# A five-stage block on one core: every hardware loop written out, and three PSUM banks each for scores and for transposes in the decayed attention

## The reference

```python
x = x + attn_a(_layernorm(x), ...)   # mamba2: projection, conv of 4 taps, silu, state-space scan, gated rmsnorm
x = x + ffn(_layernorm(x), ...)      # 2 x (local attention, windows of 64, 8 heads of 64; gated MLP, hidden 341)
x = x + attn_b(_layernorm(x), ...)   # full attention, 16 heads of 8, scores times a distance decay
x = x + ffn(_layernorm(x), ...)      # the same weights again
```

```python
scores = jnp.einsum('bhsd,bhtd->bhst', q, k) / jnp.sqrt(D)        # 512 x 512 a head
scores = scores * jnp.exp(-jnp.abs(distance_decay[0]) * dist)
out = jnp.einsum('bhst,bhtd->bhsd', jax.nn.softmax(scores, axis=-1), v)
```

## Time and profile before

| what | value |
|---|---|
| time, median of 3 runs | 2386.45 us (2385.03 to 2386.71) |
| profiled execution, its time | 2385.01 us |
| its span on the core | 2383.2 us |
| mean granted TensorE clock | 0.97 |
| instructions | 60302 |
| busy shares of the span | PE 92%, PEld 63%, DVE 68%, ACT 63%, POOL 70% |
| parts in the trace (us from the start) | mamba to 293, t0 to 1045, decayed attention to 1636, t1 to the end |

### The profile page before, as it was taken

One profiled execution on the slowest core, in us unless ns is written; L12 is line 12 of the kernel. 1 busy time (PEld: TensorE's weight loads), 2 busy tenths in 40 slices (PEclk: granted clock), 3 DMA queues, 4 the chain that ended last, 5 costly groups with the idle time before them and its releaser, 6 DMA issues. The chain is left out here.

```text
span 2383.2 us, 60302 instructions
## 1 busy us (share of the span) xinstructions
PE 2184.3 (92%) x19744; PEld 1490.5 (63%) x19760; DVE 1627.2 (68%) x3905; ACT 1489.7 (63%) x4130; POOL 1679.1 (70%) x1712
## 2 busy tenths in 40 slices
PE   6998789998989999859999999998999978999979
PEld 4766557776557777535655656564777755677755
DVE  5777578886557777537666667675878745777755
ACT  3556368887358887325655556554888843888853
POOL 5777788886168888228777777766889822888842
PEclk8999899999999999889999999998999999999999
DMA  4000011111111111112111111101111112111101
GB/s 111 1 0 1 6 27 34 40 37 30 48 36 36 36 34 33 27 58 58 54 42 34 52 53 37 49 21 25 28 34 40 43 23 51 36 34 36 39 21 50
DMA packets 121250, 86.69 MB, mean 36 GB/s; under 512 B 85560, under 2 KB 102160, under 8 KB 118800
## 3 DMA queue, kind: packets, MB, share of 16 engines
q1 hardware_dynamic: 119248, 82.70, 14.3%
q10 hardware_dynamic: 1856, 2.23, 0.3%
HBM read 30.38 MB, written 8.39 MB: 16 GB/s over the span
## 5 line engine op out<-in xcount | busy, mean ns | idle before, releaser
L1319 DVE CUSTOM_DVE_ANT_0 store<-bank,store 128x512 f32<-128x512 f32 x512 | 340.1, 689 | 170.2 <-PE bank L1165 108.6
L1403 POOL TENSOR_SCALAR store<-store 128x512 f32<-128x512 f32 x512 | 349.7, 694 | 149.5 <-DVE store L1319 147.4
L1276 ACT ACTIVATE store<-bank 128x512 f32<-128x512 f32 x512 | 287.1, 603 | 251.2 <-PE bank L1174 247.7
L730 ACT ACTIVATE store<-bank,store 128x128 f32<-128x128 f32 x1024 | 364.2, 378 | 68.5 <-DVE store L860 68.4
L1010 POOL TENSOR_TENSOR store<-store 128x16 f32<-128x16 f32 x128 | 372.5, 2910 | 26.6 <-DVE store L856 26.6
L1004 POOL TENSOR_TENSOR store<-store 128x512 f32<-128x512 f32 x256 | 321.0, 1275 | 85.0 <-DVE store L847 83.7
L1174 PEld LDWEIGHTS bank<-store 128*128 128x128 f32 x2048 | 241.4, 142 | 130.4 <-ACT store L1276 74.1
L1174 PE MATMUL bank<-store 128*128 128x128 f32 x2048 | 298.3, 278 | 0.0
L519 PE MATMUL bank<-store 128*128 128x512 f32 x512 | 270.1, 615 | 7.1 <-DVE store L835 6.6
L1019 POOL TENSOR_TENSOR store<-store 128x512 f32<-128x512 f32 x256 | 261.5, 1043 | 17.4 <-POOL store L1010 11.4
L860 DVE TENSOR_REDUCE store<-bank 128x4 f32<-128x512 f32 x256 | 165.0, 686 | 130.4 <-PE bank L553 130.4
(11 more groups left out here) (199 smaller groups left out, 4457.3 us busy)
## 6 DMA issues: line engine op xcount, KB each, us to landing
store<-store SPq DMA_DIRECT2D x256, 128.0 KB, 2.3
store<-parts SPq DMA_DIRECT2D x96, 192.0 KB
parts<-store SPq DMA_DIRECT2D x16, 384.0 KB, 3.6
store<-store SPq DMA_DIRECT2D x128, 32.0 KB
store<-store SPq DMA_DIRECT2D x128, 31.8 KB
store<-store SPq DMA_DIRECT2D x32, 127.0 KB
store<-in_L_ffn_wqkv_dram SPq DMA_DIRECT2D x4, 768.0 KB, 4.6
out_dram<-store SPq DMA_DIRECT2D x8, 256.0 KB, 2.5
```

The source lines that it names most:

```text
L730: last = nc.scalar.activation(prob[:, e, b, :], bank[3 + e][:, b * P:(b + 1) * P], ACT.Exp, bias=nmax[:, e, b:b + 1], accum_out=psums[:, h ...
L1276: nc.scalar.activation(AT[:, h % 4, c, :], bank[2 + c][:, :], ACT.Exp, scale=-1.0).then_inc(aexp_done, 1)
L1319: nc.vector.tensor_tensor_reduce(out=S[:, h % 4, t, :], in0=bank[t % 2][:, :], in1=decay[:, off:off + L], scale=1.0, scalar=-3.0e38, op0=A ...
L1403: nc.gpsimd.tensor_scalar(s_, s_, -1.0, amax[:, h % 4, t:t + 1], ALU.mult, ALU.add).then_inc(shifted_done, 1)
```

## The change

All `Fori` loops on all engines become Python loops: the same instructions in the same order on each engine, with constants in place of registers, no register arithmetic and no branches, in a program that is several times longer. In the decayed attention the six banks that scores and turns share are divided three and three in place of two and four: score n waits for scale n-3, turn n for exp n-3. The tile's bank is now its running number modulo 3. Nothing else is moved, added or taken out. The diff, cut to one loop of each kind and all of the bank edits:

```diff
@@ -322,6 +322,7 @@
         PREP_LOADS = 8
         MAMBA_LOADS, FOLD_LOADS = 11, 3
         COMBOS = 2 * PARTS
+        SCORE_BANKS, TURN_BANKS = 3, 3
         HALF = HA // 2 * L
         FIRST = 2 * TPS
         LN_START, LN_STEPS = 2 - (B - 1), B - 1
...
@@ -348,7 +349,7 @@
         credits = ((exp_done, 2), (pT_done, 2), (wo_added, 1), (rot_done, 2), (roped_done, 4),
                    (qkT_done, 2), (v_ready, 1), (o_done, SLOTS), (ss_done, 1), (xT_done, TPS),
                    (hidden_ready, 2), (down_added, 1),
-                   (scaled_done, 2), (aexp_done, TPS), (at_done, 16), (ao_ready, 1), (av_out, TPS),
+                   (scaled_done, SCORE_BANKS), (aexp_done, TURN_BANKS), (at_done, 16), (ao_ready, 1), (av_out, TPS),
                    (xt_ready, 1), (lt_ready, 1), (mm_ready, 1), (mixed, 1), (gT_ready, 1), (fuse_added, 1))
 
         def start_pool(pool):
...
@@ -479,7 +480,7 @@
                         stage_shifted(sp, 0, q0, j)
                     meet(sp, 2 * l + meets)
                     load_ff(sp, l)
-                with sp.Fori(0, B - 1) as s:
+                for s in range(0, B - 1):
                     if l == 0:
                         sp.wait_ge(ln_ready, B * norm + s + 2)
                     for j in range(TPS):
...
@@ -677,7 +678,7 @@
                 for i in range(2):
                     project_qk(q0, 2, i)
                 attention_sequence(q0, False, True)
-                with pe.Fori(1, B - 1) as s:
+                for s in range(1, B - 1):
                     attention_sequence(q0 + s, True, True)
                 attention_sequence(q0 + (B - 1), True, False)
                 weigh_values(q0 + (B - 1), TPS - 1)
...
@@ -1064,17 +1065,17 @@
                 finish_qk(q0, 0)
                 finish_qk(q0, 1)
                 if l == 0:
-                    with pool.Fori(0, B - 2) as s:
+                    for s in range(0, B - 2):
                         attention_sequence(s, q0 + s, True, True)
                     attention_sequence(B - 2, q0 + (B - 2), True)
                 else:
-                    with pool.Fori(0, B - 1) as s:
+                    for s in range(0, B - 1):
                         attention_sequence(s, q0 + s, True)
                 attention_sequence(B - 1, q0 + (B - 1), False)
                 ff_rstd(q0, 0)
                 ff_rstd(q0 + 1, 1)
                 meet(pool, l * 2 + meets + 1)
-                with pool.Fori(0, B - 2, 2) as s:
+                for s in range(0, B - 2, 2):
                     for odd in range(2):
                         ff_rstd(q0 + s + 2 + odd, odd)
                         if last_layer:
...
@@ -1162,7 +1163,7 @@
                     pe.wait_ge(combos_in[1], (q + 1) * (16 * COMBOS))
                 h, t = k // TPS, k % TPS
                 pe.wait_ge(scaled_done, 64 * q + k + 1)
-                nc.tensor.matmul(bank[t % 2][:, :], QC[0:COMBO, h, t * P:(t + 1) * P], KC[0:COMBO, h, :],
+                nc.tensor.matmul(bank[(64 * q + k) % SCORE_BANKS][:, :], QC[0:COMBO, h, t * P:(t + 1) * P], KC[0:COMBO, h, :],
                                  start=True, stop=True).then_inc(score_done, 1)
 
             def turn(q, h, c):
...
@@ -1171,12 +1172,12 @@
                     pe.wait_ge(shifted_done, 64 * q + 4 * h + 4)
                 pe.wait_ge(aexp_done, 64 * q + 4 * h + c + 1)
                 for t in range(TPS):
-                    last = nc.tensor.transpose(bank[2 + c][:, t * P:(t + 1) * P], S[:, h % 4, t, c * P:(c + 1) * P], ident)
+                    last = nc.tensor.transpose(bank[SCORE_BANKS + (64 * q + 4 * h + c) % TURN_BANKS][:, t * P:(t + 1) * P], S[:, h % 4, t, c * P:(c + 1) * P], ident)
                 last.then_inc(at_done, 1)
 
             def weigh(q, g, c):
 
-                pe.wait_ge(aexp_done, 64 * q + 16 * g + c + 17)
+                pe.wait_ge(aexp_done, 64 * q + 16 * g + c + 13 + TURN_BANKS)
                 if c == 0:
                     pe.wait_ge(ao_ready, 4 * q + g + 1)
                     if g == 0:
...
@@ -1273,7 +1274,7 @@
                     act.wait_ge(at_done, 64 * q + 4 * h + c + 17)
                     if h % 4 == 0:
                         act.wait_ge(av_out, 16 * q + h + c + 1)
-                    nc.scalar.activation(AT[:, h % 4, c, :], bank[2 + c][:, :], ACT.Exp, scale=-1.0).then_inc(aexp_done, 1)
+                    nc.scalar.activation(AT[:, h % 4, c, :], bank[SCORE_BANKS + (64 * q + 4 * h + c) % TURN_BANKS][:, :], ACT.Exp, scale=-1.0).then_inc(aexp_done, 1)
 
             def copy_oT(q, g):
                 act.wait_ge(av_out, 16 * q + 4 * g + 8)
...
@@ -1316,7 +1317,7 @@
                 dve.wait_ge(score_done, 64 * q + 4 * h + t + 1)
                 hold(dve)
                 off = (TPS - 1 - t) * P
-                nc.vector.tensor_tensor_reduce(out=S[:, h % 4, t, :], in0=bank[t % 2][:, :], in1=decay[:, off:off + L],
+                nc.vector.tensor_tensor_reduce(out=S[:, h % 4, t, :], in0=bank[(64 * q + 4 * h + t) % SCORE_BANKS][:, :], in1=decay[:, off:off + L],
                                                scale=1.0, scalar=-3.0e38, op0=ALU.mult, op1=ALU.max,
                                                accum_out=amax[:, h % 4, t:t + 1]).then_inc(scaled_done, 1)
 
...
@@ -1363,7 +1364,7 @@
 
             nc.vector.memset(bank[6][:, :], 0.0)
             sequence(0, False, True, True)
-            with dve.Fori(1, B - 2) as q:
+            for q in range(1, B - 2):
                 sequence(q, True, True, True)
             sequence(B - 2, True, True)
             sequence(B - 1, True, False, False, True)
...
@@ -1397,7 +1398,7 @@
                     nc.gpsimd.tensor_tensor(apart[:, t, 2, :], arest[:, t, :], apart[:, t, 1, :], ALU.subtract).then_inc(apart_ready, 1)
 
             def subtract_max(q, h, t):
-                pool.wait_ge(scaled_done, 64 * q + 4 * h + t + 3)
+                pool.wait_ge(scaled_done, 64 * q + 4 * h + t + 1 + SCORE_BANKS)
                 hold(pool)
                 s_ = S[:, h % 4, t, :]
                 nc.gpsimd.tensor_scalar(s_, s_, -1.0, amax[:, h % 4, t:t + 1], ALU.mult, ALU.add).then_inc(shifted_done, 1)
```

28 lines of the change are left out of this document (14 added, 14 removed).

## The result

| what | before | after |
|---|---|---|
| time, median (range) | 2386.58 us (2385.03 to 2388.57), 4 runs | 2357.37 us (2353.88 to 2359.44), 4 runs |
| profiled execution, its span | 2385.01, 2383.2 us | 2358.81, 2357.0 us |
| instructions | 60302 | 54563 |

The changed kernel takes 0.9876 of the time before (95% interval 0.9859 to 0.9893), 29.2 us less. The prediction was 2361 us, 2347 to 2376. Lines of kernel.py after stand one further down: L1320 is the L1319 of before.

What follows compares the result with a forecast made beforehand. Outside the mamba PE's queue was taken as the bound, so only its idle time could come back: 9.2 + 5.9 + 14.4 - 2.3 - 1.5 = 25.7 us off 2385.0, giving 2359.3; as a median 2361, range 2347 to 2376.

Steps and rivals of the forecast that it cites:

- DVE's loop edge: Decayed attention: DVE's four jumps back delay the next score 1.91 us each; written out, 7.6 us gained, 9.2 with clock.
- The clock part: Decayed attention: PE's clock stood at 0.57 of full for 4.0 us after the last edge; 1.6 us counted as gain.
- POOL's registers: Transformer's attention: POOL works out wait values late; written out, 3.9 us gained in second layers, 2.0 in first, 5.9 together.
- MLP 0, SP 0: MLP's loops gain nothing because PE has no idle time; SP's gain nothing because its DMAs land well ahead.
- Mamba 0, within 1: Mamba's loops: written-out sequences have the same chain of small steps, so 0 gain, with 1 us on either side.
- The banks: Decayed attention: third score bank gains 14.4 us of PE waits; one turn bank less costs 2.3 us (1.5 to 6).
- Long code: Straight-line code makes some starts late, mostly in the decayed attention: a loss of 1.5 us, between 0 and 4.
- the case's own range: Whole kernel, main forecast: banks 11 to 16, loops 12 to 17, losses 2 to 8 us, giving 2352 to 2372.
- A third bank of no use: Rival, decayed attention: DVE is full where PE waits, so only the loops' gain is left, 2375 us; chance 0.10.
- Register work counts for more: Rival, attention stages: sequencers cause all remaining PE stalls, about 20 us more gain over 28 sequences, 2341 us; chance 0.08.
- ACT's pace: Rival, decayed attention: exps at 0.5 us against turns at 0.44 bound the turns, losing 23 us, 2384; chance 0.05.
- Code fetch: Rival, long code: PE gaps with no releaser every 10 to 15 us would show it; chance 0.05.

Runs made afterwards that it cites:

- the leaner kernel: Changed kernel's banks, but only nine loops written out (decayed PE, ACT, DVE; POOL's transformer attention; mamba's four): 2354.58 us, ratio 0.9863 to the kernel before.
- the repeat: The changed kernel measured once more with nothing altered: 2355.92 us, ratio 0.9869 to the kernel before.

## Why the prediction was right

**DVE's loop edge**, 7.6 us and 1.6 of clock. Right in mechanism and size: 2.0 us an edge against 1.91, and 8.5 us by the medians of the run with this edit alone. The clock part was one execution's, as the traces with 70.0 to 70.6 us in all four looped sequences show; without it the term is 7.6 to 8.

**POOL's registers**, 5.9 us. The second layers' 0.28 us a sequence is exact (34.11 to 33.83). The first layers' half share of it, a guess without a row, measured 0.13 to 0.16, which was luck; it was taken for 14 sequences, where the loops there hold 12, 0.3 us too much. The four layers: 1495.4 to 1497.1 us in the seven traces with POOL's loop, 1490.0 to 1492.2 in the seven with it written out, on average 5.2 us less.

**MLP 0, SP 0.** Rounds of 8.27 us in both. SP's loops were not tried alone; the run that keeps them (the leaner kernel) is no slower.

**Mamba 0, within 1.** Written out, its four looped sequences fall from 31.07 and 30.88 in turn to 30.74: 0.9 us, at the edge of the bound. Something else is in the traces that was not foreseen: some sequences take 32.1 to 32.5 us. Windows of the run with POOL's attention loops alone, over its second sequence, 32.3 us long, and over an undisturbed one (columns as in the earlier trace rows):

```profile
93.40:125.70 32.30, 29.27 (x169) 22.81 (x168) 24.08 (x49) 18.25 (x41) 24.20 (x41) 0.95 0.00 1
...
222.20:253.00 30.80, 27.82 (x170) 21.41 (x170) 21.99 (x46) 18.23 (x41) 22.57 (x39) 1.00 0.00 1
```

The granted clock is 0.95 there, and 1.00 in the other. But the clock alone does not make it: in the run with two and three banks it is 0.94 over sequences that take 30.75 us. In the eight traces with the mamba written out such a sequence is at most the first (five of eight); in the five whose mamba was looped there are 0, 2, 5, 2 and 0, at any of the first five places. That would fit written-out code keeping PE steadier; but the medians with and without the mamba's loops (2378.6 and 2377.3) do not show it, so it stays open.

**The banks**, 14.4 - 2.3 = 12.1 us. Measured 12.3 on top of DVE's edge, and 14.1 on top of all loops, from first to last turn. What stays of PE's waits is 1.5 us in two, as 1.4 had been left. The turn's wait stands where it was put and is as long as it was put, 0.21 us in head 5 and in no other head; that this alone is 2.3 us a stage was too much, 1.0 with two score banks and at most 1.7 with three. So the score banks alone, put at 14.4, gave 13 to 14 us on top of DVE's edge and 15 to 16 on top of all loops, and that the net came out within 0.2 us of the first is in part luck.

**Long code**, 1.5 us, between 0 and 4. The block count was wrong: 159, not 134, since the share of repeated time is not the share of repeated instructions. The cost is in the lower part of the bounds: one late start of 0.36 us a stage on DVE, and no difference that shows against a kernel with 68 blocks less. One thing is not explained: with all loops written out but two score banks a decayed sequence takes 68.3 us where it takes 68.12 with DVE's loop alone, in steps of 0.04 to 0.08 us at heads 5, 12 and 13, where a score begins that much later behind its scale. With three banks it vanishes (66.63 in both). Which engine's loop it hangs on was not tried.

**The sum** was 25.4 us on the medians and 29.2 were measured (30.0 in the repeat). In the decayed attention, first to last turn, the traces give 22.8 us against the one of before, and 21.0 and 21.5 against the two others with the same decayed code; forecast were 21.3, less the part of the long code. In the transformer they give 5.0 to 6.1. Errors cancelled in the sum: the gain was put 1.6 us too high for the clock, and the losses too high by some 1 us for the long code and by 0.6 to 1.3 us for the turn bank. The rest is the scatter of both kernels, whose single runs spread over 2353.3 to 2359.4 and 2381 to 2397. Three slips are in the working and none decides it: the case's own range, by its parts, begins at 2355 and not at 2352 (2385.0 - 16 - 17 + 2, and 1.4); POOL's first layers have 12 looped sequences; and PE's records show 40 loop branches, not 36.

**The rivals.** A third bank of no use: excluded, 11 and 14 us by the medians. Register work counts for more: excluded, POOL's loops alone give all of it. ACT's pace: excluded at three turn banks; at two the turns do wait for ACT. Code fetch: excluded for PE. It was looked for on the wrong engine and in the wrong kind of code: not straight code on PE, but a long loop on DVE is where fetching costs, and there it costs up to 7.9 us a turn.

## What to carry to other kernels

Read a loop's edge on each engine by itself, in the trace's branch and register records: on DVE and POOL a body of 297 or 439 records stood still 2.8 to 6.4 us at each backward jump, one of 221 or fewer did not, PE's did not at any length here, and it only matters if the engine is next to the path. A time measured with such a loop in it is a time for that placement of code: an edit elsewhere in the same engine's stream can move it by 0.8%, so write the long loop out before other edits are compared. When buffers are moved from one use to another, work out the new wait head by head from the start of each producer and consumer: it found the one place of sixteen and its 0.2 us here, and for one turn bank less 3 to 6 us a sequence, of which 4.5 came. That next step is near: it turned a gain of 1.2% into a loss of 0.2%.

## What the runs showed of the hardware

**A jump back to code that is not at hand.** DVE, body of 297 records: 2.6 to 2.75 us of idle ahead of the next operation, 2.8 to 3.0 us from the branch to the next register operation, in all four turns. POOL, body of 439: 5.9 and 6.4 us. POOL with 221 and ACT with 161: 0.25 to 0.28 us. PE, whose body has some 596 records on its weight-load side alone, has none (0.27 to 0.28 us). A block of code starts to come in 1.0 to 1.1 us behind each of DVE's jumps, inside the stop. The Trainium skill, "Runtime: NRT & Kernel Launch", Instruction fetch mechanics, says that a taken branch to a target outside the two blocks on hand forces a fetch; the traces agree, in that a fetch stands in each of DVE's stops. It gives a block as 16 KiB or 256 instructions, and PE a memory four times as large. PE's blocks are of that size here (69 in 1.13 MB), those of the other engines are not: 77 in 0.63 MB, 8.2 KB each. By the page two blocks hold 512 instructions, and yet DVE's body of 297 stalled; at what length between 221 and 297 it begins was not tried.

**A second stop after the jump.** With other code ahead of it the same loop stops again 2.2 us after its restart, for 2.1 to 3.6 us, between two instructions that wait for nothing. In all eight cases a block of code (the trace does not name its engine) starts to come in 4.8 to 6.4 us behind the branch, and the stop ends 2.3 to 2.5 us after that start. In the kernel before a block comes in at 4.7 to 6.1 us as well, and DVE does not stop. So the second stop is a wait for code; that it shows only where the body begins near the end of a block, and DVE runs out of the first block too early, is argued, not shown. The same section speaks of sequential prefetch and of one stall at the branch, and not of this second one.

**Straight code.** 159 blocks on PE (2.61 MB) against 91 made no difference in the span (2354.9 us in both); on DVE one start in the decayed attention was 0.31 us late, with nothing on record that it waited for.
